# One stage for the out-projection and the FFN head of a two-layer transformer kernel, and raw weights asked for piece by piece

## The chip, the cores and the metric

The kernel runs on one core of a Trainium2 chip. The metric is device microseconds of one execution; before the change the median of three runs is 1880.46 us (1876.26 to 1881.61). One further execution was profiled: 1877.46 us, of which the span from its first to its last instruction is 1875.7 us. PE is TensorE, ACT ScalarE, DVE VectorE, POOL GpSimd; SP only issues DMAs.

## The reference, cut to what matters

Four batches of 512 tokens, width 512, fp32. Two layers, each attention and a feed-forward network (FFN). Layer 0, the projections of layer 1's attention and its softmax are not touched. What follows them is:

```
attn = attn.reshape(b, n, 512);  x = x + attn @ Wout + bout           # layer 1 attention, its end
xn = layernorm(x)
g = xn @ Wg.T;  u = xn @ Wu.T                                          # DFF = 1408 = 11 x 128
x += silu(g) * u @ Wd.T
for e in top2(softmax(xn @ Wr.T)), weight we:                          # 8 experts, rank 16
    h = silu(g + xn@Ag[e].T@Bg[e].T*2) * (u + xn@Au[e].T@Bu[e].T*2)
    x += we * (h @ Ad[e].T @ Bd[e].T * 2)
```

## The kernel before, in words

An fp32 product is made of fp32r halves: a matrix is split into HI (a rounding copy, on ACT) and LO (the rest, a subtraction on DVE or POOL), and each product takes three matmuls (HI HI, HI LO, LO HI). "A product of twelve" below is four blocks of 128 in depth times these three, 128 x 512 out. A matrix that must be turned first is turned on PE as 128 x 128 transposes, four to a PSUM bank, and ACT and DVE split it out of the bank.

The part that the change touches comes in this order.

- **Attention** (`phase_rope_attention1`, L1676). 32 groups of four heads. POOL divides each group's sums and writes them to `attn`, laid out by group (`normalise`, L1740). Wout comes in raw.
- **Out-projection** (`phase_out1`, L1968). ACT and DVE split Wout. Then, for each of 16 token tiles in a hardware loop over the batches (`pe.Fori`, L2001): ACT gathers the tile's rows out of `attn` (L2024), PE turns them, ACT and DVE split them, PE makes the product of twelve, DVE adds it to x and takes statistics.
- **FFN** (`phase_ffn1`, L2072). Small matrices (Ag, Au, Wr, Bd) are loaded, turned and split once. Then a loop over two halves of two batches each (L2244). Each half has a *head* (normalise, turn and split the eight token tiles; router; top two of the experts on DVE; masks of 128 expert-rank columns made by DVE and turned on PE by `turn_masks`, L2289; the products with Ag and Au, masked and split into `am`), 22 *steps*, and a *tail* (masks turned again, the accumulated low-rank rows masked and split, the product with Bd per tile, the output stored).
- **The steps.** A half goes through the 11 blocks f of DFF, and per block through its two batches c. A step (`tile`, L2340) on PE: product of twelve for g; transposes of one piece of block f+1's raw weights (`prep`); product of twelve for u; the previous step's down product (twelve); the low-rank additions for one expert choice (`lora`, six); another `prep`; the previous step's low-rank down product (six); `lora` of the other choice (six). ACT makes silu and HI, DVE the product with u and the sums into x, POOL LO.
- **The raw weights.** Gate, up, down and lora pieces of block f come by six DMAs on one semaphore. SP issues all six when all four pieces of the block before are turned (L2204). PE waits for all six ahead of the first of them:

```
sp.wait_ge(prep_.filled, START + (h * NF + f) * PREP)      # L2204, then six DMAs, L2205 to L2211
if part == 0:
    pe.wait_ge(raw_in, (h * NF + f + 1) * LOADS * DMA)     # L2232
```

The order on each engine is written out by hand; nothing plans it.

Of the kernel before, what the change touches and what calls it, by code (L numbers as in the profile page):

```python
# [1259 lines left out]
def phase_qkv1(nc, io, x, ident, stats, experts, early):  # L1260
# [20 lines left out]
    with ExitStack() as ctx:  # L1281
# [16 lines left out]
        wq = sb("wq", [P, 2, DK, 2, 2, P], FP32R)  # L1298
# [6 lines left out]
        sinT, cosT = sb("sinT", [P, 2, S]), sb("cosT", [P, 2, S])  # L1305
        ctxT = sb("ctxT", [P, 2, CK, S], FP32R)
        xn = sb("xn", [P, TPB, D])
        xnT = sb("xnT", [P, 2, DK, S], FP32R)
        y_in = early.y_in
        qk = sb("qk", [P, RING, 2, 2, S], FP32R)  # L1310
# [365 lines left out]
def phase_rope_attention1(nc, io, x, ident, attn, wout, early):  # L1676
# [7 lines left out]
    with ExitStack() as ctx:  # L1684
# [48 lines left out]
        @block.gpsimd  # L1733
        def _(pool):

            for s in range(early.SLOTS, RING):
                early.set_ones(nc.gpsimd, kM[s], slot_set[s], lambda done: pool.wait_ge(slot_set[s], done))
            pool.wait_ge(bout_in, DMA)

            def normalise(g):  # L1740
                pool.wait_ge(rinv_made, g + 1)
                nc.gpsimd.tensor_tensor(attn[:, g, :, :], sums[g % 2][:, :, 0:HD],  # L1742
                                        rinv[g % 2][:].unsqueeze(2).to_broadcast([P, KT * GROUP, HD]), ALU.mult).then_inc(out_done, 1)

            for g in range(GROUPS):
                if g < TILES:
                    nc.gpsimd.tensor_tensor(x[:, g, :], x[:, g, :], bout[:], ALU.add)
                normalise(g)

        @block.sync  # L1750
        def _(sp):
# [10 lines left out]
            sp.dma_start(wout.raw[:], io["L1_xattn_Wout"].rearrange("(k p) n -> p k n", p=P)).then_inc(wout.loaded, DMA)  # L1762
# [197 lines left out]
class OutWeights:  # L1960


    def __init__(self, nc, ctx):
        self.raw = ctx.enter_context(nc.sbuf_tensor("wout_raw", [P, DK, D], FP32))
        self.loaded = ctx.enter_context(nc.semaphore("wout_in"))


def phase_out1(nc, io, x, ident, stats, attn, wout):  # L1968

    from contextlib import ExitStack  # L1970
    with ExitStack() as ctx:
        def sb(name, shape, dt=FP32):
            return ctx.enter_context(nc.sbuf_tensor(f"o_{name}", shape, dt))

        def ps(name, shape):
            return ctx.enter_context(nc.psum_tensor(f"o_{name}", shape, FP32))

        def sem(name):
            return ctx.enter_context(nc.semaphore(f"o_{name}"))

        w = sb("w", [P, 2, DK, D], FP32R)
        rows = [sb(f"rows{i}", [P, D]) for i in range(2)]
        aT = [sb(f"aT{i}", [P, 2, DK, P], FP32R) for i in range(2)]
        tp = [ps(f"tp{i}", [P, D]) for i in range(2)]
        y_ps = [ps(f"y{i}", [P, D]) for i in range(2)]
        t_ = Split(nc, ctx, "ot")
        w_hi, w_split, rows_ready, y_ready, y_added = (
            sem("w_hi"), sem("w_split"), sem("rows_ready"), sem("y_ready"), sem("y_added"))
        block = ctx.enter_context(nc.Block())

        @block.tensor
        def _(pe):
            start_counts(pe, t_.filled)
            def out_product(tile, t):

                pe.wait_ge(t_.split, START + tile + 2)
                pe.wait_ge(y_added, START + tile)
                product(nc, y_ps[t % 2][:], [([aT[t % 2][:, h, k, :] for h in (HI, LO)],
                                              [w[:, h, k, :] for h in (HI, LO)]) for k in range(DK)]).then_inc(y_ready, 1)

            with pe.Fori(0, B) as b:  # L2001
                for t in range(TPB):
                    tile = b * TPB + t

                    pe.wait_ge(rows_ready, tile + 1)
                    pe.wait_ge(t_.split, START + tile)
                    transposes(nc, t_, tp[t % 2], [rows[t % 2][:, k * P:(k + 1) * P] for k in range(DK)], ident)
                    if t == 0:
                        pe.wait_ge(w_split, DK)
                    if t:  # L2010
                        out_product(tile - 1, t - 1)
                out_product(b * TPB + TPB - 1, TPB - 1)

        @block.scalar
        def _(act):
            act.wait_ge(wout.loaded, DMA)
            for k in range(DK):
                nc.scalar.activation(w[:, HI, k, :], wout.raw[:, k, :], ACT.Copy).then_inc(w_hi, 1)
            with act.Fori(0, B) as b:
                for t in range(TPB):  # L2020
                    tile = b * TPB + t

                    act.wait_ge(t_.filled, START + (tile - 1 if t else b * TPB))
                    nc.scalar.activation(rows[t % 2][:].rearrange("p (g c) -> p g c", g=HEADS // GROUP),  # L2024
                                         attn[:, ds(b * (HEADS // GROUP), HEADS // GROUP), t * GROUP:(t + 1) * GROUP, :]
                                         .rearrange("p g a c -> p g (a c)"), ACT.Copy).then_inc(rows_ready, 1)
                    split_hi(nc, act, t_, tile, aT[t % 2][:, HI], tp[t % 2][:].rearrange("p (k c) -> p k c", k=DK))

        @block.vector
        def _(dve):  # L2030
            start_counts(dve, t_.split, y_added)
            dve.sem_inc(t_.split, 1)
            dve.sem_inc(y_added, 1)
            for k in range(DK):
                dve.wait_ge(w_hi, k + 1)
                nc.vector.tensor_tensor(w[:, LO, k, :], wout.raw[:, k, :], fp32(w[:, HI, k, :]), ALU.subtract).then_inc(w_split, 1)

            def add(tile, t):
                dve.wait_ge(y_ready, tile + 1)
                nc.vector.tensor_tensor(x[:, ds(tile, 1), :], y_ps[t % 2][:].rearrange("p (a c) -> p a c", a=1),  # L2040
                                        x[:, ds(tile, 1), :], ALU.add).then_inc(y_added, 1)

            def out_stats(tile):

                dve.wait_ge(y_added, START + tile + 2)
                tile_stats(nc, stats, x, tile)

            with dve.Fori(0, B) as b:
                for t in range(TPB):
                    tile = b * TPB + t  # L2050
                    split_lo(nc, dve, t_, tile, aT[t % 2][:, LO], tp[t % 2][:].rearrange("p (k c) -> p k c", k=DK), aT[t % 2][:, HI])
                    if t >= 2:
                        out_stats(tile - 2)
                    if t:
                        add(tile - 1, t - 1)
                out_stats(b * TPB + TPB - 2)
                add(b * TPB + TPB - 1, TPB - 1)
                out_stats(b * TPB + TPB - 1)


def phase_rope1(nc, io, x, ident, stats, experts):
    from contextlib import ExitStack
    with ExitStack() as ctx:
        early = AttentionInputs(nc, ctx)
        phase_qkv1(nc, io, x, ident, stats, experts, early)
        attn = ctx.enter_context(nc.sbuf_tensor("attn", [P, GROUPS, TPB * GROUP, HD], FP32))
        wout = OutWeights(nc, ctx)
        phase_rope_attention1(nc, io, x, ident, attn, wout, early)
        phase_out1(nc, io, x, ident, stats, attn, wout)


def phase_ffn1(nc, io, x, ident, stats):  # L2072

    from contextlib import ExitStack
    ER = E1 * R1
    NF = DFF // P  # L2080
    HALVES = 2
    CH = B // HALVES
    HT, HTOK = CH * TPB, CH * S
    STEPS = NF * CH
    PREP = 4
    USES = TPB + 2
    gate_dram, up_dram, down_dram = io["L1_ffn_Wg"], io["L1_ffn_Wu"], io["L1_ffn_Wd"]
    out_dram = io["out"].rearrange("b (t p) d -> p (b t) d", p=P)
    with ExitStack() as ctx:
# [9 lines left out]
        xnT = sb("xnT", [P, 2, DK, HTOK], FP32R)  # L2099
        agT, auT = sb("agT", [P, 2, DK, ER], FP32R), sb("auT", [P, 2, DK, ER], FP32R)  # L2100
        wrT = sb("wrT", [P, 2, DK, E1], FP32R)
        bdT = sb("bdT", [ER, 2, D], FP32R)
        wr_raw = sb("wr_raw", [E1, D])
        gate_raw, up_raw, down_raw = sb("gate_raw", [P, D]), sb("up_raw", [P, D]), sb("down_raw", [P, DK, P])
        lora_raw = sb("lora_raw", [P, 3, P])
        gateT = [sb(f"gateT{s}", [P, 2, DK, P], FP32R) for s in range(2)]
        upT = [sb(f"upT{s}", [P, 2, DK, P], FP32R) for s in range(2)]
        downT = [sb(f"downT{s}", [P, 2, D], FP32R) for s in range(2)]
        loraT = [sb(f"loraT{s}", [P, 2, 3, P], FP32R) for s in range(2)]
        rl = sb("rl", [P, S])  # L2110
        logits = sb("logits", [P, HT, E1])
        shifted = sb("shifted", [P, HT, E1])
        rev = sb("rev", [P, HT, E1])
        hots = sb("hots", [P, HT, 4, E1])
# [575 lines left out]
```

## Time and profile before

| | us |
|---|---|
| median of three runs | 1880.46 |
| the profiled execution | 1877.46 |
| its span | 1875.7 |
| PE busy | 1663.6 (89%) |
| DVE busy | 1111.9 (59%) |
| ACT busy | 819.4 (44%) |
| POOL busy | 430.0 (23%) |
| mean granted TensorE clock | 0.941 of full |

The busy shares are averages over stages that differ. The table is read only to see which engine leads; what a stage is bound by stands in its own windows, in the waits ahead of PE, and in the order of PE's instructions. "PEld" is the loading of stationary operands, which overlaps the matmuls. Idle time of an engine that is not the last one in a stage costs nothing.

### The profile page before, as it was taken

The numbers are of one execution on the slowest core, as the hardware profiler recorded it, in microseconds if no ns is written. First come the engines' busy times: TensorE is split into PE (matmuls) and PEld (weight loads), VectorE is DVE, ScalarE is ACT, GpSimd is POOL, SyncE is SP. The second block draws the span as 40 slices with busy tenths as digits, with TensorE's granted clock in tenths as the row PEclk, the third lists the DMA queues.
The fourth block names the chain that finished last, engine by engine and source line by source line (L and its number), as shares of the span: only waits on it lengthen the run. The fifth ranks groups of instructions, "written<-read, shape, count | busy, mean of one in ns | idle before, by whom it ended". The sixth has DMA issues, their size and how long they took to land. (4 is left out here: it accounts for less than half of the span.)

```text
span 1875.7 us, 27784 instructions
## 1 busy us (share of the span) xinstructions
PE 1663.6 (89%) x8787; PEld 1220.7 (65%) x8787; DVE 1111.9 (59%) x1999; ACT 819.4 (44%) x1304; POOL 430.0 (23%) x394
## 2 busy tenths in 40 slices
PE   6978599999578869999999896899999888999997
PEld 5767599999456623334333374687778657778785
DVE  5876522222277668888988354554555565555555
ACT  4653223333244328777788722433333324333332
POOL 1210122222256621111000000322222203232221
PEclk8999599999788859999999897999999989999998
DMA  8995045742347542222222002011110030110101
GB/s 289 341 347 176 29 155 177 264 173 80 114 150 235 162 137 69 70 69 69 70 69 69 2 0 60 22 39 25 42 42 21 1 88 22 42 42 21 42 21 45
DMA packets 135840, 182.56 MB, mean 97 GB/s; under 512 B 62560, under 2 KB 83040, under 8 KB 130864
## 3 DMA queue, kind: packets, MB, share of 16 engines
q1 hardware_dynamic: 129488, 160.65, 27.3%
q0 software_dynamic: 6240, 20.45, 3.2%
q8 instruction: 65, 1.06, 0.2%
q14 instruction: 47, 0.39, 0.1%
HBM read 253.41 MB, written 61.21 MB: 168 GB/s over the span
## 5 line engine op out<-in xcount | busy, mean ns | idle before, releaser
L1926 DVE TENSOR_REDUCE r_top<-r_ring 128x1 f32<-128x512 f32 x512 | 324.1, 681 | 34.2 <-PE r_ring L1823 29.8
L1909 ACT ACTIVATE r_probs<-r_st 128x1024 f32<-128x1024 f32 x256 | 248.1, 1022 | 48.1 <-PE r_st L1810 45.5
L2482 POOL TENSOR_TENSOR f_hidS<-f_work,f_hidS 128x512 fp32r<-128x512 f32 x132 | 170.6, 1293 | 416.8 <-ACT f_hidS L2442 416.8
L48 PE MATMUL m_bank<-w_place,m_xT 128*128 x936 | 168.2, 329 | 3.4 <-DVE m_xT L1189 3.1
L2599 DVE TENSOR_TENSOR f_work<-f_work,f_u 128x512 f32<-128x512 f32 x132 | 90.8, 688 | 133.9 <-PE f_u L48 74.0
L2437 ACT ACTIVATE f_work<-f_g 128x512 f32<-128x512 f32 x132 | 79.0, 598 | 182.7 <-PE f_g L56 125.7
L48 PEld LDWEIGHTS m_bank<-w_place,m_xT 128*128 128x128 f32 x936 | 153.5, 191 | 7.7 <-issue 4.3
L2442 ACT ACTIVATE f_hidS<-f_work 128x512 fp32r<-128x512 f32 x132 | 83.4, 632 | 169.3 <-DVE f_work L2599 169.3
L1844 PE MATMUL r_out<-r_probs,early_v 128*17 128x512 f32 x1024 | 135.6, 601 | 0.5 <-ACT r_probs L1909 0.4
L48 PE MATMUL f_u<-f_xnT,f_upT 128*128 128x512 f32 x528 | 131.7, 398 | 0.0
L48 PE MATMUL f_g<-f_xnT,f_gateT 128*128 128x512 f32 x528 | 126.9, 389 | 0.0
L48 PE MATMUL f_y<-f_downT,f_hidS 128*128 128x512 f32 x528 | 126.8, 389 | 0.0
L1823 PE MATMUL r_ring<-early_slots 48*128 48x512 f32 x256 | 108.2, 507 | 17.3 <-PEq L1281 12.7
L2581 DVE TENSOR_TENSOR x_tokens<-f_y,x_tokens 128x512 f32 x176 | 120.2, 692 | 0.0
L48 PEld LDWEIGHTS f_g<-f_xnT,f_gateT 128*128 128x128 f32 x528 | 99.1, 188 | 20.7
L48 PEld LDWEIGHTS f_y<-f_downT,f_hidS 128*128 128x128 f32 x528 | 99.1, 188 | 20.6
L1823 PEld LDWEIGHTS r_ring<-early_slots 48*128 48x128 f32 x256 | 44.9, 196 | 99.0 <-DVE r_top L1926 81.2
L48 PEld LDWEIGHTS f_u<-f_xnT,f_upT 128*128 128x128 f32 x528 | 96.2, 188 | 19.0
L1823 PE MATMUL r_ring<-r_kM,r_qS 48*128 48x512 f32 x256 | 104.1, 476 | 3.0 <-DVE r_top L1926 0.7
L1194 DVE TENSOR_TENSOR m_hT<-m_bank,m_hT 128x384 fp32r<-128x384 f32 x39 | 21.8, 558 | 137.8 <-ACT m_hT L1027 105.7
L1823 PEld LDWEIGHTS r_ring<-r_kM,r_qS 48*128 48x128 f32 x256 | 43.0, 187 | 85.5 <-DVE r_top L1926 78.9
L1742 POOL TENSOR_TENSOR attn<-r_sums,r_rinv 128x256 f32<-128x256 f32 x32 | 19.9, 621 | 343.3 <-DVE r_rinv L1942 343.3
(345 smaller groups left out, 3024.2 us busy)
## 6 DMA issues: line engine op xcount, KB each, us to landing
w_place<-expert_split SPq DMA_DIRECT2D x72, 1408.0 KB
w_place<-expert_split SPq DMA_DIRECT2D x36, 1024.0 KB
expert_split<-w_place SPq DMA_DIRECT2D x10, 1408.0 KB, 8.9
w_place<-expert_split SPq DMA_DIRECT2D x36, 384.0 KB
early_slots<-y_rows SPq DMA_DIRECT2D x16, 512.0 KB, 6.0
k_split<-q_qk SPq DMA_DIRECT2D x32, 256.0 KB
q_split<-q_qk SPq DMA_DIRECT2D x32, 256.0 KB
w_raw<-in_L_ffn_down_proj SPq DMA_DIRECT2D x8, 704.0 KB, 7.2
```

What stands on the lines that cost most here:

```text
L48: last = nc.tensor.matmul(out, l, r, start=(i == 0), stop=(i == len(passes) - 1))
L1194: nc.vector.tensor_tensor(hT[:, i % 2, LO], bank[1][:, 0:FT * P].rearrange("p (j c) -> p j c", j=FT), fp32(hT[:, i % 2, HI]), ALU.subtract ...
L1742: nc.gpsimd.tensor_tensor(attn[:, g, :, :], sums[g % 2][:, :, 0:HD], rinv[g % 2][:].unsqueeze(2).to_broadcast([P, KT * GROUP, HD]), ALU.mu ...
L1823: nc.tensor.matmul(ring(place(q, h))[:], qS[s][rows, h // 2, q * P:(q + 1) * P], kM[s][rows, h // 2, :], start=True, stop=True).then_inc(m ...
L1844: last = nc.tensor.matmul(out_ps[h * PAD:h * PAD + VCOLS, :], v[:, k, g, h * VCOLS:(h + 1) * VCOLS], probs[k][:, h, :], start=(k == 0), st ...
L1909: nc.scalar.activation(probs[k][:, 2 * pair:2 * pair + 2, :], st_ps[pair][:], ACT.Exp, scale=SCALE).then_inc(exp_done, 1)
L1926: nc.vector.reduce_max(top[g % 2][:, q, h:h + 1], ring(place(q, h))[:], AXIS_X).then_inc(max_read, 1)
L2437: nc.scalar.activation(hid(c, var), g_ps[c][:], ACT.Silu).then_inc(silu_done, 1)
L2442: nc.scalar.activation(hidS[c][:, var, HI, :], hid(c, var), ACT.Copy).then_inc(hid_hi, 1)
L2482: nc.gpsimd.tensor_tensor(hidS[c][:, var, LO, :], hid(c, var), fp32(hidS[c][:, var, HI, :]), ALU.subtract).then_inc(hid_split, 1)
L2581: nc.vector.tensor_tensor(x[:, at, :], ring(c, i)[:].rearrange("p (a c) -> p a c", a=1), x[:, at, :], ALU.add).then_inc(y_added, 1)
L2599: nc.vector.tensor_tensor(hid(c, var), hid(c, var), u_ps[c][:], ALU.mult).then_inc(hid_done, 1)
```

## The change

Three things are rearranged; the arithmetic stays.

1. **Storage.** `attn`, raw Wout and split Wout are allocated ahead of the QKV phase, whose temporaries now lie in them. `attn` is laid out by token tile, so POOL writes each group to its final place and no gather on ACT is left. POOL also splits Wout, in groups 16 to 19 of the attention.
2. **One stage `phase_out_head`** over four batches in the order 2, 3, 0, 1, unrolled, software-pipelined by batch: iteration j has batch j's out-projection, batch j-1's normalisation, router and choice, and batch j-2's masks and Ag/Au products. POOL normalises. A mask is now a product of the chosen rows with a 32 x 128 selection matrix (six matmuls of 512 columns a batch) instead of 32 transposes a half, twice. Batches 2 and 3 have their turned xn and `am` (2 MB each) stored to DRAM, all batches the two masks of the tail. The first block's raw weights are turned at the end.
3. **One stream of 44 steps.** `phase_ffn1` starts at the first g product and goes on from half 0 to half 1 without a head; SP loads xn and `am` of batches 2 and 3 back over those of 0 and 1. The tail's masked delta (`make_delta`, `delta_rows`) of batches 0 and 1 lies inside steps 22 to 25; raw pieces have a semaphore each, and each is asked for when its own predecessor is turned.

```diff
+class FfnState:
+    ORDER = (2, 3, 0, 1)
...
-            def load(h, f):
-                sp.wait_ge(prep_.filled, START + (h * NF + f) * PREP)
...
+            for part in range(late.PARTS):
+                late.load_raw(sp, 1, part)
+            load_mask(0)
+            for w in range(1, SLOTS_W - 1):
+                for part in range(late.PARTS):
+                    sp.wait_ge(prep_turned, (w - 1) * late.PARTS + part + 1)
+                    late.load_raw(sp, w + 1, part)
+                if w == NF - 1:
+                    load_rows(0)
+                    load_rows(1)
+                if w == NF:
+                    load_mask(1)
+                if w == NF + 1:
+                    load_mask(2)
+                    store_rows(0, 0, TPB)
+                if w == NF + 2:
+                    store_rows(1, 0, TPB)
+            store_rows(2, 0, TPB)
+            load_mask(3)
...
+            def load_rows(c):
+                last = STEPS_H - CH + c
+                sp.wait_ge(up_ready, 3 * last + 1)
+                sp.dma_start(fp32(late.xnT[:, c].rearrange("p h k n -> p (h k n)")), late.x_dram[c]).then_inc(x_in[c], DMA)
+                sp.wait_ge(up_ready, 3 * last + 3)
+                sp.dma_start(fp32(late.am[:, c].rearrange("p i k h n -> p (i k h n)")), late.am_dram[c]).then_inc(am_in[c], DMA)
```

PE's order in the new stage (left out under `j == 0` are four transposes of the constants, `turn_const`, and under `j == B` the four `prep` of the first block):

```diff
+            turn_rows(0, 0)
+            turn_rows(0, 1)
+            for j in range(B + 2):
+                if j < B:
+                    out_product(j, 0)
+                    turn_rows(j, 2)
+                    out_product(j, 1)
+                    turn_rows(j, 3)
+                    out_product(j, 2)
+                    out_product(j, 3)
+                if j == 0:
...
+                if j == B:
...
+                if 1 <= j <= B:
+                    for t in range(TPB):
+                        turn_x(j - 1, t)
+                if j >= 2:
+                    turn_hots(j - 2)
+                if 1 <= j <= B:
+                    router(j - 1)
+                if j >= 2:
+                    masks(j - 2)
+                if 1 <= j <= B:
+                    turn_logits(j - 1)
+                if j + 1 < B:
+                    turn_rows(j + 1, 0)
+                    turn_rows(j + 1, 1)
+                if j >= 2:
+                    lora_rows(j - 2)
```

ACT follows the same order: `row_hi`, `normed_hi` x 4, `deviation` (Sqrt), `hot_rows_hi`, `copy_router`, `copy_masks` x 4, `gaps` (Exp), `row_hi` x 2 of the next batch, `masked_hi` x 4. DVE: `add`, `add_stats` and `row_lo` of the four tiles, `variance`, `normed_lo` x 4, `hot_rows_lo`, `reciprocals`, `route` (the top two, a chain of some twenty small operations), `row_lo` x 2, `mask_rows` x 4. PE's end of the steps:

```diff
+            down(STEPS - 1, SLOTS_W - 1, CH - 1)
+            delta_rows(CH)
+            down_lora(STEPS - 1, SLOTS_W - 1, CH - 1, TPB)
+            delta_rows(CH + 1)
```

## Rows read from the trace of the kernel before

**Rows 1.** Windows by stage: stretch, length, busy (count) per engine, clock, DMA share, GB/s.

```profile
1064.00:1129.00 65.00, 55.45 (x256) 44.40 (x256) 34.69 (x52) 20.07 (x36) 0.00 (x0) 0.92 0.00 0
1129.00:1179.40 50.40, 35.10 (x175) 25.43 (x176) 26.68 (x86) 18.18 (x35) 1.02 (x1) 0.80 0.26 56
1179.40:1484.10 304.70, 292.70 (x1339) 238.59 (x1337) 164.00 (x245) 105.27 (x177) 91.99 (x71) 0.99 0.13 29
1484.10:1505.00 20.90, 12.50 (x57) 8.74 (x56) 13.65 (x21) 5.41 (x10) 0.00 (x0) 0.84 0.08 31
1505.00:1545.00 40.00, 31.14 (x160) 22.54 (x161) 23.10 (x56) 13.40 (x28) 1.04 (x1) 0.87 0.32 88
1545.00:1849.30 304.30, 292.45 (x1339) 238.47 (x1337) 164.01 (x245) 105.26 (x177) 92.00 (x71) 0.99 0.13 29
1849.30:1875.70 26.40, 12.48 (x56) 8.74 (x56) 14.31 (x22) 4.13 (x9) 0.00 (x0) 0.81 0.21 80
```

**Rows 2.** Waits: engine, line, for what: us in all, times, longest.

```profile
PE f_prep L143 <- DMA f_lora_raw<-in_L_ffn_Ad: 13.6, 18, 1.0
```

**Rows 3.** Windows of the two steps of one block.

```profile
1575.47:1589.49 14.02, 13.43 (x64) 10.84 (x62) 7.30 (x11) 4.79 (x9) 3.88 (x3) 1.00 0.22 46
1589.49:1602.57 13.08, 13.08 (x63) 10.81 (x61) 7.16 (x11) 4.64 (x9) 3.87 (x3) 1.00 0.10 31
```

**Rows 4.** Timeline of SP: start, us, instruction; first and last DMA of a block.

```profile
1627.52 0.35 SPq L2205 DMA_DIRECT2D f_gate_raw<-in_L_ffn_Wg  x1
...
1630.70 1.32 SPq L2211 DMA_DIRECT2D f_lora_raw<-in_L_ffn_Ad  x1
```

**Rows 5.** Timeline of PE in the same block, idle time before in brackets.

```profile
1629.92 2.88 PE L48 MATMUL f_g<-f_xnT,f_gateT 128*128 128x512 f32 x12
1633.56 0.65 PE L143 MATMUL f_prep<-identity,f_gate_raw 128*128 128x128 f32 x4 [0.76 <-DMA f_lora_raw<-in_L_ffn_Ad]
```

**Rows 6.** Timeline of PE, first step of half 0.

```profile
1190.66 1.62 PE L56 MATMUL f_g<-f_am,f_loraT 128*128 128x512 f32 x3 [5.14 <-DVE f_work L2599]
...
1196.95 2.91 PE L48 MATMUL f_g<-f_xnT,f_gateT 128*128 128x512 f32 x12
```

**Rows 7.** Timeline of PE in the out-projection.

```profile
1070.06 4.76 PE L48 MATMUL o_y<-o_w,o_aT 128*128 128x512 f32 x12
1074.66 0.60 PE L143 MATMUL o_tp<-identity,o_rows 128*128 128x128 f32 x4
1075.02 3.00 PE L48 MATMUL o_y<-o_w,o_aT 128*128 128x512 f32 x12
...
1078.21 5.74 PE L48 MATMUL o_y<-o_w,o_aT 128*128 128x512 f32 x24
1083.79 0.60 PE L143 MATMUL o_tp<-identity,o_rows 128*128 128x128 f32 x4
...
1098.24 0.60 PE L143 MATMUL o_tp<-identity,o_rows 128*128 128x128 f32 x4
```

**Rows 8.** Timeline of DVE: one LO split; first and last operation of a choice.

```profile
1145.54 0.69 DVE L134 TENSOR_TENSOR f_xnT<-f_g,f_xnT 128x512 fp32r<-128x512 f32 x1 [0.47 <-ACT f_xnT L128]
...
1163.69 0.18 DVE L2509 COPY f_logits<-f_u 128x32 f32<-128x32 f32 x1
...
1169.59 0.22 DVE L2544 TENSOR_TENSOR f_hots<-ft_hot,ft_w 128x64 f32<-128x64 f32 x1
```

**Rows 9.** Groups of instructions: busy us, mean ns, idle before.

```profile
L2471 POOL TENSOR_TENSOR f_am<-f_work,f_am 128x512 fp32r<-128x512 f32 x8 | 11.9, 1511 | 181.3 <-ACT f_am L2429 181.3
L97 ACT ACT_TABLE_LOAD x1 | 1.3, 1283 | 6.9 <-PEq L1971 6.9
```

**Rows 10.** A window of layer 0 in which DMA loads run back to back.

```profile
270.00:275.00 5.00, 5.00 (x30) 4.58 (x30) 1.77 (x3) 1.67 (x4) 0.97 (x1) 1.00 0.99 377
```

**Rows 11.** Timeline of PE at the end of the kernel.

```profile
1845.06 2.88 PE L48 MATMUL f_y<-f_downT,f_hidS 128*128 128x512 f32 x12
```

**Rows 12.** The output's stores (1 MB each), from issue to landing.

```profile
DMA to landing us min/median/max: 4.3/4.4/5.4
```

More of the change, by code:

```diff
@@ L1991, in _, with turn @@
         @block.tensor
         def _(pe):
[L1993 to L2001, printed above, removed]
-                for t in range(TPB):
[L2003 to L2012, printed above, removed]
+            def turn(bank, ins, done):
+                at = 0
+                for a in ins:
+                    n_rows, n_cols = a.shape[0], a.shape[1]
+                    last = nc.tensor.transpose(bank[0:n_cols, at:at + n_rows], a, ident[0:n_rows, 0:n_rows])
+                    at += n_rows
+                last.then_inc(done, 1)
@@ L2014, in _, with row_hi @@
         @block.scalar
         def _(act):
[L2016 to L2019, printed above, removed]
-                for t in range(TPB):
[L2021 to L2027, printed above, removed]
+            def row_hi(j, t):
+                act.wait_ge(rows_turned, TPB * j + t + 1)
+                wait_count(act, y_ready, TPB * j + t - 1)
+                nc.scalar.activation(aT[:, t % 2, HI], tp[t % 2][:].rearrange("p (k c) -> p k c", k=DK), ACT.Copy).then_inc(rows_hi, 1)
@@ new lines, in gaps, with masked_hi @@
+            def gaps(j):
+                act.wait_ge(gap_ready, j + 1)
+                nc.scalar.activation(shifted[:], shifted[:], ACT.Exp).then_inc(gap_exp, 1)
+                nc.scalar.activation(top.e[:], top.gap[:], ACT.Exp).then_inc(gap_exp, 1)
+            def masked_hi(j):
+                c = j % 2
+                for q in range(4):
+                    act.wait_ge(a_masked, 4 * j + q + 1)
+                    if j >= 2:
+                        act.wait_ge(am_out[c], DMA)
+                    nc.scalar.activation(late.am[:, c, q // 2, q % 2, HI, :], work[:, q, :], ACT.Copy).then_inc(am_hi, 1)
@@ L2179, in tiles @@
[L2179 to L2189 removed]
+        mask_in, acc_clear = sem("mask_in"), sem("acc_clear")
+        z_ready, z_hi, z_split, stored = sem("z_ready"), sem("z_hi"), sem("z_split"), sem("stored")
@@ new lines, in prep, with ring_wait @@
+            def prep(f, part):
+                pe.wait_ge(late.raw_in[part], (f + 1) * late.LOADS[part] * DMA)
+                wait_count(pe, prep_split, (f - 1) * late.PARTS + part)
+                ins, _, _ = late.part(f, part)
+                for k, a in enumerate(ins):
+                    last = nc.tensor.transpose(prep_ps[:, k * P:(k + 1) * P], a, ident[:])
+                last.then_inc(prep_turned, 1)
+            def ring_wait(use):
+                wait_count(pe, y_added, use - 2)
@@ new lines, in _ @@
+            for step in range(STEPS):
+                w, c = step // CH, step % CH
+                if w == NF:
+                    pe.wait_ge(x_in[c], DMA)
+                wait_count(pe, prep_split, w * late.PARTS)
+                wait_count(pe, hid_done, 3 * (step - 1))
+                product(nc, g_ps[c][:], [([late.gate(w, h, k) for h in (HI, LO)], [late.xnT[:, c, h, k, :] for h in (HI, LO)])
+                                         for k in range(DK)]).then_inc(gate_ready, 1)
+                if w + 1 < SLOTS_W:
+                    prep(w + 1, 2 * c)
+                product(nc, u_ps[c][:], [([late.up(w, h, k) for h in (HI, LO)], [late.xnT[:, c, h, k, :] for h in (HI, LO)])
+                                         for k in range(DK)]).then_inc(up_ready, 1)
+                if step:
+                    down(step - 1, (step - 1) // CH, 1 - c)
+                lora(step, w, c, 1)
+                if w + 1 < SLOTS_W:
+                    prep(w + 1, 2 * c + 1)
+                if step:
+                    down_lora(step - 1, (step - 1) // CH, 1 - c)
+                if step > STEPS_H and z_made(step - 1) is not None:
+                    delta_rows(z_made(step - 1))
+                lora(step, w, c, 2)
```

1081 lines of the change are left out of this document (597 added, 484 removed).

## The prediction

> **What bounds the kernel now.** I read the windows by stage first [rows 1]. In the two step stretches (304.7 and 304.3 us) PE is busy 292.7 and 292.5 us at clock 0.99: PE bounds them, and only its gaps can go. In the out-projection, the two heads and the two tails PE is busy 55.5 of 65.0, 35.1 of 50.4, 31.1 of 40.0, 12.5 of 20.9 and 12.5 of 26.4 us, at clocks of 0.80 to 0.92: there chains through ACT and DVE end last. Then the waits: PE stands 18 times for the raw weights [rows 2]. Of a block's two steps the one that waits takes 14.02 us, the other 13.08 [rows 3]; they hold the same 54 matmuls and eight against seven transposes (0.12 us by the 0.36 from four transposes to the next product [rows 7]), so a wait costs 0.85 to 1.0 us with its restart. The cause is in the order of issue: the six DMAs start at 1627.52, the last is issued at 1630.70, PE needs them at 1632.8 [rows 4, 5].
>
> **The raw weights.** Each piece is now asked for when its predecessor is turned, a whole block (26 us) before it is needed. The wait goes 18 times: 18 x 0.99 = **-18**. Without the wait PE is next: its matmuls follow at once in the step that has no wait. Bounds: -13.6 (the idle time alone [rows 2]) to -19.
>
> **First step.** Before it takes from 1179.4 to 1196.95, 17.5 us [rows 1, 6], with PE waiting 5.14 us because DVE is still masking and splitting `am`. Now `am` is ready. I count g 4.7 (slow clock after the barrier, as 1070.06 to 1074.66 [rows 7]), prep 0.4, u 2.8, DVE's product 1.2, lora 1.4, prep 0.4, silu and product of the second choice 0.7, lora 1.4: 13. **-4.5** (bounds -7 to 0).
>
> **Between the halves.** Removed: the last step's down part of half 0, 4.1 us (12 + 6 matmuls), the tail 20.9, and the first step of half 1, which ends as the other did, 17.4: 42.4. The head (40.0) is counted below. Added: a full step, 13.2; eight raw pieces' work that block 10 now has, 1.8; two deltas of twelve matmuls, 5.6; 0.5 for DVE, which has four adds and a mask more in steps 22 to 25 (7.2 us busy of 13.1 now [rows 3], about 12 then). And a new wait. SP is in order: for `load_rows(1)` it waits until step 21's last up product, the very end of half 0, issues 2 MB of `am`, and only then asks for block 12's gate piece. PE wants that piece 2.8 us into step 22. Loads run at up to 377 GB/s [rows 10], so 2.1 MB take 5.6 us, plus issue and landing (PE had a block's pieces 2.1 us after the last issue [rows 4, 5]): 9 us after the step's start, a wait of 6, and 1.9 for the slow clock after it (4.6 instead of 2.8 for a product [rows 7]): 8. Sum 29, so **-13**. Bounds of the new wait: 0 (the piece overtakes) to 16 (behind x and `am` both). The xn and `am` loads themselves have 13 to 21 us each and are hidden by the steps.
> The Trainium skill, DMA: Bandwidth & Descriptors (Anatomy of one DMA), gives 2.0 us + bytes / 436 GB/s for a DMA on another issue path, as an estimate 6.8 us for 2.1 MB; by it the wait would be 5 instead of 6.
>
> **The new stage against the old out-projection and heads.** Old: 1064.0 to 1179.4 and 1505 to 1545, 155.4 us. New, by following PE's order and its waits:
> - Start: no Wout split and no gather, first product 3 us in instead of 6. Products of batch 0: four at 2.8 and two turns at 0.36, 12, and 1.9 for the slow first: 14.
> - Gap to batch 1: DVE has add, statistics, variance, the four constants' LO and the reciprocals ahead of `row_lo`: 5.8.
> - Batch 1: products 12. Then turn_x: the first two at once, the others only when DVE, held by add, statistics and variance for 2.5 us, has split two tiles (ACT, then DVE, 0.69 for DVE's half [rows 8]); router from 6.0, ending 8.8; logits copied and turned by 10.2; the choice on DVE 6.1 before ([rows 8], 64 columns; 32 now); `row_lo` 0.7, next product at 17.4. With the clock down after 6 idle us, 1.9: 31.3.
> - Batch 2: the same, with masks (2.0, as the fourth waits for a copy) and lora_rows (24 matmuls, 5.5) filling the choice's time: 12 + 18.5 = 30.5.
> - Batch 3: 12, 11.2 to the logits, 5.5 lora_rows: 28.7.
> - j = 4: ACT is busy with `masked_hi` until 4 us later, so prep stalls 5 us; prep and turn_x end at 11.8, router 4.7 at the slow clock, masks and logits 2.4, lora_rows 5.5: 24.4.
> - j = 5, nothing beside it: choice 1, hots turned, split and multiplied 5.9, lora_rows 7 at a clock partly low, masking 1.5, HI 1, POOL's two LO at 1.5 [rows 9] 3: 19.9. Barrier 0.9.
>
> Sum 158.5, **+3**. The old stage's 16 transposes of masks a half, twice, and 2.4 us a batch lost at each loop turn (14.45 from 1083.79 to 1098.24 against 12.0 [rows 7]) do go; what takes their place is a serial chain a batch (split, router, choice, split) with only two batches' work to lie beside it. PE's work here is about 98 us at full clock; it is idle for the rest. Bounds: 140 (chains shorter, gaps filled) to 183 (the 12.3 us of PE work behind each batch's chain at half clock, and 1 us more in each hand-over).
> Hidden, and what it costs without cover: POOL's Wout split (8 operations, up to 1.5 us [rows 9], POOL nearly idle in the attention); stores of 9 MB (no engine waits, except for mask buffers); four more Sqrt and four Exp loads on ACT, 1.28 us each [rows 9], which fall where ACT waits anyhow; 10 us if all were exposed. The attention itself I leave at 0, -1 to +2.
> The Trainium skill, ScalarE: Activation LUTs (What ACT_TABLE_LOAD costs), puts a switch at 2.66 us with a drain; eight exposed would be 21. By rows 9 the load takes 1.28. This is the page's rule that speaks against the change.
>
> **Tail.** Old: 30.6 from the last down product at 1845.06 to the end [rows 11]. New: down 2.7; make_delta(2) 4.4, during which PE idles; delta 4.7 at the slow clock; down_lora 1.4. Then mask 3, whose load SP issues only behind the 1 MB store of batch 2, lands about 15.5 after the down product; delta chain 3.5, product 4.7, last add, store (4.4 a MB [rows 12], less for a quarter) and end 4.5. Sum 2.7 + 28 = 30.7: **0** (-4 to +4).
>
> **Sum** against the profiled execution: -18 - 4.5 - 13 + 3 + 0 = -32.5; 1877.5 - 32.5 = 1845. That execution is 3.0 us below the median of the three runs, inside their spread; I put the median at **1846**.
>
> **Rivals.**
> - *The stage's chains overlap better* than I follow them (140 to 148 us): 1832. For it: DVE is busy 0.53 and ACT 0.31 of the old stages [rows 1]. Against: DVE's own order puts `route` ahead of `row_lo`.
> - *The reload holds longer*: xn and `am`, 8 MB through one queue while raw pieces wait behind; each block boundary at 11 and 12 loses 8 more: 1860. For it: SP is in order. Against: the loads are spread over 26 us.
> - *The change doesn't do what it says for the raw weights*: the wait was PE's own pipeline at the piece's turn, not the data. Then -18 is lost: 1864. Against: the step with two preps and no wait takes 13.08.
> - *Slower*: the new stage runs at 1.2 GHz. Its PE use after each batch's products is under half for 12 us, and the old head shows 0.80 [rows 1] with a product of twelve at 4.6 instead of 2.8 after a pause [rows 7]. If the clock stays low through whole batches, the 84 us of PE work after batch 0 take up to 84 more, of which I put 45 on the path: 1891. It decides from 35 us on. Against: the old out-projection, with 1.8 us gaps each batch, keeps the full clock.
>
> **Chances.** Forecast (1836 to 1856) 0.55, better overlap 0.16, longer reload 0.12, no gain on raw weights 0.06, slow clock 0.05, other mishaps between 1860 and 1880 0.06. The range 1829 to 1866 takes in the first three and most of the fourth. About 0.3% (5.6 us) is what a measurement here tells from no change: faster 0.92, same 0.03, slower 0.05.
>
> **What would show it.** Raw weights: no PE wait for `lora_raw`, 26.3 us a block instead of 27.1 to 27.4. Reload: one wait of 5 to 8 us of PE for a gate piece in step 22, none for xn. Stage: 150 to 165 us from the attention's last transposes to the first g, PE idle 4 to 7 us ahead of each `out_product(j, 0)` for j = 1, and at `turn_x(j, 2)`. Tail: DVE idle 4 us for mask 3. Wrong: a stage under 145 or over 170 us, or blocks that still take 27.

## The result, and the profile after

The changed kernel takes 1845.9 us (median of four runs, 1844.3 to 1850.5) beside 1881.0 for the kernel before (1876.3 to 1881.7): ratio 0.9822, 95% interval 0.9806 to 0.9838. The forecast was 1846, range 1829 to 1866. Timed again later, beside the experiments, the ratio was 0.9794 (0.9773 to 0.9815), 1847.2 against 1885.0.

The profiled execution is the slowest of the four: 1850.5 us, span 1848.7. Its windows by stage (stretch, length, busy per engine with count, clock, DMA share, GB/s) answer to [rows 1]:

```profile
1068.33:1225.84 157.51, 124.72 (x551) 90.64 (x552) 77.62 (x213) 53.63 (x99) 32.13 (x33) 0.87 0.22 79
1225.84:1239.68 13.84, 12.57 (x44) 9.62 (x45) 2.76 (x4) 5.28 (x8) 5.44 (x3) 0.78 0.50 140
1239.68:1515.76 276.08, 276.08 (x1292) 228.14 (x1291) 151.78 (x231) 97.92 (x169) 82.19 (x64) 1.00 0.21 58
1515.76:1537.22 21.46, 15.27 (x63) 12.31 (x62) 7.31 (x11) 4.78 (x9) 3.88 (x3) 0.84 0.46 144
1537.22:1569.24 32.02, 32.02 (x149) 26.11 (x147) 26.51 (x38) 10.37 (x19) 8.37 (x6) 1.00 0.39 114
1569.24:1817.17 247.93, 247.93 (x1155) 204.96 (x1153) 134.88 (x205) 86.66 (x149) 73.51 (x57) 1.00 0.15 35
1817.17:1848.70 31.53, 15.09 (x43) 10.87 (x41) 15.52 (x23) 2.01 (x4) 1.57 (x2) 0.73 0.24 83
```

They are the joined stage, the first step, steps 1 to 21, step 22 (the first of the second half), steps 23 and 24 with their deltas, the rest of the steps, the tail. In three of them (276.08, 32.02, 247.93 us) PE's busy time equals the length; in [rows 1] the two step stretches had 12 us of gaps each. The waits of PE from the attention's end on (line, for what: us in all, times, longest) have no `lora_raw` any more [rows 2]; what is left is the stage, the reload, the barrier ahead of the first g (`f_g`, 5.0) and the tail. The seven largest are:

```profile
PE f_ring L48 <- DVE wout_split L2777: 13.3, 2, 9.2
PE h_y L48 <- DVE late_weights L2405: 7.9, 3, 4.8
PE h_tp L2171 <- DVE late_xnT L2434: 7.3, 4, 2.0
PE f_prep L2632 <- DMA wout_raw<-in_L_ffn_Wg: 6.2, 1, 6.2
PE f_g L48 <- PEq L2059: 5.0, 1, 5.0
PE h_tp L2234 <- issue: 3.8, 1, 3.8
PE h_y L2171 <- DVE late_weights L2501: 3.1, 1, 3.1
```

The two steps of a block, read from where PE starts each step's g (timeline, start and length), take 13.21 and 13.08 us, 26.29 a block, against 14.02 and 13.08 [rows 3]:

```profile
1608.62 2.89 PE L48 MATMUL f_g<-late_xnT,late_weights 128*128 128x512 f32 x12
1621.83 2.88 PE L48 MATMUL f_g<-late_xnT,late_weights 128*128 128x512 f32 x12
1634.91 2.89 PE L48 MATMUL f_g<-late_xnT,late_weights 128*128 128x512 f32 x12
```

The reload at the change of half, SP's requests and then PE:

```profile
1508.80 0.32 SPq L2588 DMA_DIRECT2D late_xnT<-late_x_dram  x1
1515.96 0.32 SPq L2590 DMA_DIRECT2D late_am<-late_am_dram  x1
1516.32 0.69 SPq L2042 DMA_DIRECT2D wout_raw<-in_L_ffn_Wg  x1
```

```profile
1515.76 2.88 PE L48 MATMUL f_g<-late_xnT,late_weights 128*128 128x512 f32 x12
1524.84 1.12 PE L2632 MATMUL f_prep<-identity,wout_raw 128*128 128x128 f32 x4 [6.19 <-DMA wout_raw<-in_L_ffn_Wg]
1525.60 4.50 PE L48 MATMUL f_u<-late_xnT,late_weights 128*128 128x512 f32 x12
```

SP asks for the gate piece only after the second `am`, which waits for the last product that reads its buffer. PE wants the piece 2.7 us into step 22, gets it 6.19 us later, and runs the next product of twelve in 4.50 us instead of 3.0. From its request to PE's start the piece takes 8.5 us, with 2 MB of `am` ahead of it in the same queue; the 21 gate pieces of the kernel take 2.4 us at least, 2.6 in the median and 8.5 at most, this one (DMA issues: count, KB, median us from issue to landing):

```profile
wout_raw<-in_L_ffn_Wg SPq DMA_DIRECT2D x21, 256.0 KB, 2.6
```

The spans differ by 27.0 us. The milestones of both traces (attention's last turn, first g, end of the first step, last down product, end) divide that among the prediction's terms:

| stretch | predicted | measured |
|---|---|---|
| up to the attention's end | 0 | +4.1 |
| joined stage against out-projection and first head | +43.1 | +42.3 |
| first step | -4.5 | -3.7 |
| first step's end to last down product | -71.3 | -70.6 |
| tail | +0.1 | +0.9 |
| sum | -32.6 | -27.0 |

The second and fourth lines hold one move: the second half's head (40.0 us) was forecast inside the stage and leaves the steps, so +3 is 43.1 - 40.0, and -71.3 is -18 (waits) - 42.4 - 40.0 + 29.1.

### The profile page after: what moved, and what is told of

It reads as the page before. It is cut to its first block and busy times, and to the rows that moved or that the text cites. A ratio compares the mean times of both kernels' runs of the same rounds, so it can differ in the third digit from the quotient of the medians.

```text
span 1848.7 us, 25581 instructions
## 1 busy us (share of the span) xinstructions
PE 1657.8 (90%) x8699; PEld 1217.9 (66%) x8699; DVE 1088.1 (59%) x2001; ACT 808.5 (44%) x1283; POOL 458.6 (25%) x425
## 5 line engine op out<-in xcount | busy, mean ns | idle before, releaser
L1937 DVE TENSOR_REDUCE r_top<-r_ring 128x1 f32<-128x512 f32 x512 | 324.1, 682 | 35.8 <-PE r_ring L1834 31.5
L2719 ACT ACTIVATE attn<-f_g 128x512 f32<-128x512 f32 x132 | 79.1, 599 | 192.1 <-PE f_g L56 132.2
L2793 DVE TENSOR_TENSOR attn<-attn,f_u 128x512 f32<-128x512 f32 x132 | 90.8, 688 | 121.4 <-PE f_u L48 67.0
L2748 POOL TENSOR_TENSOR wout_split<-attn,wout_split 128x512 fp32r<-128x512 f32 x66 | 85.8, 1300 | 215.2 <-ACT wout_split L2723 215.2
L2748 POOL TENSOR_TENSOR f_hidS<-attn,f_hidS 128x512 fp32r<-128x512 f32 x66 | 85.7, 1298 | 204.2 <-ACT f_hidS L2723 204.2
L48 PE MATMUL f_g<-late_xnT,late_weights 128*128 128x512 f32 x528 | 129.6, 395 | 5.0 <-PEq L2059 5.0
L48 PE MATMUL f_u<-late_xnT,late_weights 128*128 128x512 f32 x528 | 133.6, 402 | 0.0
L2761 DVE TENSOR_TENSOR x_tokens<-f_ring,x_tokens 128x512 f32<-128x512 f32 x176 | 120.2, 692 | 0.0
L48 PEld LDWEIGHTS f_g<-late_xnT,late_weights 128*128 128x128 f32 x528 | 100.7, 191 | 26.5 <-issue 5.4
L48 PEld LDWEIGHTS f_u<-late_xnT,late_weights 128*128 128x128 f32 x528 | 97.3, 191 | 19.4
L48 PE MATMUL m_bank<-w_place,m_hT 128*128 (+1 forms) x351 | 90.8, 403 | 1.4 <-DVE m_hT L1194 1.4
```

The costliest lines, as they stand in the source:

```text
L48: last = nc.tensor.matmul(out, l, r, start=(i == 0), stop=(i == len(passes) - 1))
L1937: nc.vector.reduce_max(top[g % 2][:, q, h:h + 1], ring(place(q, h))[:], AXIS_X).then_inc(max_read, 1)
L2719: nc.scalar.activation(hid[:, c, var, :], g_ps[c][:], ACT.Silu).then_inc(silu_done, 1)
L2748: nc.gpsimd.tensor_tensor(hidS[c][:, var, LO, :], hid[:, c, var, :], fp32(hidS[c][:, var, HI, :]), ALU.subtract).then_inc(hid_split, 1)
L2761: nc.vector.tensor_tensor(x[:, at, :], ring(use)[:], x[:, at, :], ALU.add).then_inc(y_added, 1)
L2793: nc.vector.tensor_tensor(hid[:, c, var, :], hid[:, c, var, :], u_ps[c][:], ALU.mult).then_inc(hid_done, 1)
```

## The experiments

Times are medians; "before" is 1885.0 in the first group of four (17 runs), 1885.0 in the second (9) and 1885.6 in the third (9). The changed kernel was timed in the second group (1847.2); runs of the other groups are compared with it too, as "before" agrees within 0.6 us.

**e1_pieces_only.** The kernel before, with the raw weights' part of the change alone (SP's loop over the blocks is unrolled for it).

```
- sp.wait_ge(prep_.filled, START + (h * NF + f) * PREP)      # all four turned
- sp.dma_start(gate_raw ...).then_inc(raw_in, DMA); ...      # six, one semaphore
+ turned(0); sp.dma_start(gate_raw ...).then_inc(raw_in[0], DMA)
+ turned(1); sp.dma_start(up_raw ...).then_inc(raw_in[1], DMA)
+ ...
```

> The kernel before, with one part of the change alone: the six raw low-rank pieces of an FFN step are asked for one by one, each with its own semaphore, as their buffers come free. If the 13.6 us for which TensorE stood ahead of the first prep product, 18 times, was the landing of pieces asked for too late, 17 to 18 steps lose about 1 us each: 16 to 19 us faster than before, about 1863. The rival, that the 1 us was TensorE's own pipeline or the VectorE copies and not the transfer, gives 0: about 1880.

1862.8 us (1861.0 to 1867.0), ratio 0.9887 (0.9861 to 0.9912): 22 us faster. PE waits for no lora piece, and its steps start 13.21 and 13.09 us apart, as in the changed kernel:

```profile
1566.95 2.89 PE L48 MATMUL f_g<-f_xnT,f_gateT 128*128 128x512 f32 x12
1580.16 2.89 PE L48 MATMUL f_g<-f_xnT,f_gateT 128*128 128x512 f32 x12
1593.25 2.89 PE L48 MATMUL f_g<-f_xnT,f_gateT 128*128 128x512 f32 x12
```

From the first low-rank product to the last down product the profile has 1828.10 - 1192.14 = 635.96 us, against 1845.06 - 1190.66 = 654.40 before [rows 6, 11]: 18.4. So the wait was the data, and it was worth 18 in that execution; the medians gave 22, above the 16 to 19 expected.

**e2_pieces_undone, e2_second_look.** The changed kernel with that part undone.

```
- for part in range(late.PARTS):
-     sp.wait_ge(prep_turned, (w - 1) * late.PARTS + part + 1)
-     late.load_raw(sp, w + 1, part)
+ sp.wait_ge(prep_turned, w * late.PARTS)
+ for part in range(late.PARTS):
+     late.load_raw(sp, w + 1, part)
```

PE waits for all four pieces ahead of the first, at the reload too.

> The changed kernel with that one part undone: the six raw pieces are asked for together once all four pieces of the step have been turned, and TensorE waits for all of them ahead of the first prep product. Theory: 19 to 21 us slower than the changed kernel, about 1866 (one such wait per step again). Rival, that the gain of the whole change came from the joined stage and the better overlap: 0 to 5 us slower, about 1848.

1880.8 us (14 runs, 1868.6 to 1886.2): 34 us slower than the changed kernel, more than any theory had. The rival is out, but the size was open. The profile (1868.6, the fastest of the 14) loses 26.3 us in its steps: 607.80 against 581.49 from first low-rank to last down product. Of these 23.7 are waits for the pieces. The one at the reload is 8.91 us instead of 6.19, and the other 18 in that stretch sum to 20.9, 1.16 each, where the kernel before has 0.76 each [rows 2]; those of the second half are the longer ones (0.90 to 2.11 us, against 0.50 to 1.09). So undoing the part costs more here than it won there. A second profile was taken for the rest; the steps of the first, "about 604" below, are 607.80 us as measured:

> A second profile of the kernel in which the raw pieces are asked for together. Its first profile lay 12 us under the median of its times, and the steps of that profile lost 26 us against the changed kernel's, while the medians differ by 33. If the short waits also cost clock in some executions, a slower profile has blocks with a granted clock under 1.00 (or products of twelve over 2.9 us) in the steps; if the rest is of the stages before, the steps take again about 604 us and the difference lies ahead of them.

1874.8 us, steps 610.96: 3.2 more than the first. The waits are the same in sum; the first profile's, then the second's:

```profile
PE f_prep L2634 <- DMA wout_raw<-in_L_ffn_Ad: 30.7, 20, 8.9
```

```profile
PE f_prep L2634 <- DMA wout_raw<-in_L_ffn_Ad: 30.3, 20, 8.9
```

The clock is not. The same step in the two, with the wait in brackets and the product after it:

```profile
1705.53 0.63 PE L2634 MATMUL f_prep<-identity,wout_raw 128*128 128x128 f32 x4 [2.11 <-DMA wout_raw<-in_L_ffn_Ad]
1705.91 3.01 PE L48 MATMUL f_u<-late_xnT,late_weights 128*128 128x512 f32 x12
```

```profile
1707.32 0.63 PE L2634 MATMUL f_prep<-identity,wout_raw 128*128 128x128 f32 x4 [2.01 <-DMA wout_raw<-in_L_ffn_Ad]
1707.70 4.58 PE L48 MATMUL f_u<-late_xnT,late_weights 128*128 128x512 f32 x12
```

A stall of 2 us cost 1.6 us of slow product besides in one execution and nothing in the other; in the second profile it happened twice (again after a wait of 2.11 us), which is 3.1 of the 3.2. So the clock theory holds for these 3.2 us. The median is 6 us above even this profile, and that rest has not been seen in a trace. It stays open.

**before_second_look.** The kernel before, profiled again.

> A second profile of the kernel before, for the same question: taking its 18 waits away alone won 22 us by the medians, 18 by the length of its steps. If short waits cost clock in some executions, the two step stretches take more than 304.7 and 304.3 us here and show a granted clock under 0.99; if not, they take 304 to 305 again.

1885.6 us. The windows of the steps behind each half's first step have a clock of 1.00 in both profiles, so here the clock theory fails; but the steps take 1852.81 - 1192.75 = 660.06 us, 5.7 more than in the first profile, and the waits are longer than in [rows 2]:

```profile
PE f_prep L143 <- DMA f_lora_raw<-in_L_ffn_Ad: 18.7, 18, 1.3
```

Neither theory of this expectation named that: the time until the pieces are there differs between executions (0.52 to 0.94 us of wait at the first block, 0.89 to 1.31 at the fourth). Against this profile e1 wins 24.1 us in its steps, against the first 18.4; its median lies between.

**e3_reload_order.** SP's order at the reload.

```
- if w == NF - 1: load_rows(0); load_rows(1)      # x0, am0, x1, am1
- (next turn of the loop) raws(NF, (0, 1, 2, 3))
+ load_x(0); raws(NF, (0, 1)); load_am(0); raws(NF, (2,)); load_x(1); raws(NF, (3,)); load_am(1)
```

> The changed kernel with the order of SyncE's requests changed at the reload of the gate's second-half weights: each raw gate or up piece is asked for ahead of the store or accumulator load that waits for a late product, where its buffer is already free. In the changed kernel TensorE stood 6.19 us for the reloaded piece, and the step after it ran 21.46 us against 13.2. Theory, a request held up behind others in SyncE's order: 7 to 9 us faster, about 1838. Rival, that the transfer itself or the accumulators' loads are what comes last: 0 to 2 us.

1837.2 us (1836.1 to 1842.0), ratio 0.9749 (0.9727 to 0.9771), 10.0 under the changed kernel's 1847.2. The gate piece is now asked for 20 us ahead of the step and before `am` (SP, then PE), and step 22 runs through at full clock in 13.21 us (21.46 before the edit):

```profile
1491.50 0.34 SPq L2588 DMA_DIRECT2D late_xnT<-late_x_dram  x1
1491.89 0.43 SPq L2042 DMA_DIRECT2D wout_raw<-in_L_ffn_Wg  x1
1496.02 0.33 SPq L2044 DMA_DIRECT2D wout_raw<-in_L_ffn_Wu  x1
1498.78 0.33 SPq L2593 DMA_DIRECT2D late_am<-late_am_dram  x1
```

```profile
1511.68 2.89 PE L48 MATMUL f_g<-late_xnT,late_weights 128*128 128x512 f32 x12
1514.40 0.60 PE L2644 MATMUL f_prep<-identity,wout_raw 128*128 128x128 f32 x4
1514.76 3.00 PE L48 MATMUL f_u<-late_xnT,late_weights 128*128 128x512 f32 x12
...
1524.89 2.88 PE L48 MATMUL f_g<-late_xnT,late_weights 128*128 128x512 f32 x12
```

From the first step's end to the last down product: 569.2 us against 577.5. The 8.3 us came from when the piece was asked for and what lay ahead of it in the queue; the `am` load itself, which nothing sped up, stays hidden. This run doesn't tell the two apart: how much a faster `am` transfer would have won in the old order was not tested.

**e4_mask_early.** The last mask goes into an accumulator that is already free, ahead of the stores.

```
+ sp.wait_ge(z_split, 1)
+ sp.dma_start(down_acc[:, 0] ..., late.mask_dram[3]).then_inc(mask3_in, DMA)
  store_rows(2, 0, TPB)
- load_mask(3)
```

> The changed kernel with the last mask loaded early into an accumulator buffer that is already free, on a semaphore of its own, so that the tail doesn't wait for it. In the profile VectorE stood 4.95 us for that mask, and TensorE's last delta product 9.18 us behind VectorE. Theory, the mask is on the path that sets the end: 5 to 6 us faster, about 1840. Rival, that the stores of the last blocks or the split of the down delta come last at once behind it: 0 to 1 us.

1841.7 us (1836.7 to 1843.8), ratio 0.9767 (0.9746 to 0.9788). In the changed kernel's tail (VectorE, then PE):

```profile
1836.59 0.69 DVE L2772 TENSOR_TENSOR attn<-attn 128x512 f32<-128x512 f32 x1 [4.95 <-DMA attn<-late_mask_dram]
...
1840.09 5.49 PE L48 MATMUL f_ring<-late_bdT,wout_split 128*128 128x512 f32 x12 [9.18 <-DVE wout_split L2777]
```

and in this one:

```profile
1827.24 4.60 PE L48 MATMUL f_ring<-late_bdT,wout_split 128*128 128x512 f32 x12 [4.34 <-DVE wout_split L2782]
```

The tail takes 1835.0 - 1809.13 = 25.9 us against 31.5, 5.7 less, 0.9 of it the shorter delta product; the medians give 5.5. The mask was what came last.

**after_again.** The changed kernel, as the measure.

> The changed kernel itself, unaltered, as the measure for the kernels run beside it. The ratio to the kernel before should come out at 0.98 again. Its profile tells whether the 4.1 us by which the end of attention (work that the change doesn't touch) lay later in the first profile was of that one execution: then attention should end at 1062 to 1063 us here; if it is of the change, again at 1066.

1847.2 us. Attention ends at 1062.1 us here, and between 1060.5 and 1067.6 in the profiles of the other experiments, none of which touches it: the 4.1 us of the table's first line belong to the one execution. Everything behind it repeats within 0.3 us here (stage 157.26, steps 577.41). The stage doesn't do so always: in the profiles of e2 (two), e3, e4 and e7, which leave it as it is, it takes 154.64, 157.39, 156.76, 153.79 and 157.40 us. In the two short ones (154.64 and 153.79) the same products run in less time; the third of the four routers, for one, takes 2.94 and 3.38 us instead of 5.28.

**e5_rows_first.** VectorE's order in the stage's second round, and ScalarE's with it (`gaps` and `row_hi` are ScalarE's).

```
- gaps(0); row_hi(2, ...); route(0); row_lo(2, ...)
+ row_hi(2, ...); gaps(0); row_lo(2, ...); route(0)       # for j == 1 alone
```

> The changed kernel with one edit in the joined stage: in the second round of its loop VectorE makes the next batch's row halves ahead of the gaps and the routing of the batch before. In the changed kernel TensorE stood 7.9 us in 3 waits for these halves (4.80 us ahead of batch 2's product). Theory, it is VectorE's order: 3.5 to 6 us faster than the changed kernel. Rival, that routing then comes late and TensorE waits for the turned x halves instead, or the time is only the clock's: 0, or 1 to 2 us slower.

1841.0 us (1838.7 to 1844.1), 6.2 faster; the stage takes 150.53 us against 157.26. Batch 2's first product in the changed kernel (second profile), then here:

```profile
1115.29 5.49 PE L48 MATMUL h_y<-wout_split,late_weights 128*128 128x512 f32 x12 [4.79 <-DVE late_weights L2405]
```

```profile
1111.30 3.03 PE L48 MATMUL h_y<-wout_split,late_weights 128*128 128x512 f32 x12 [0.97 <-DVE late_weights L2407]
```

Of the 6.7 us, 3.8 are the wait and 2.5 this product's clock. PE waits nowhere for the routing after it. The rival's clock is thus a part of the gain, behind the wait. Which of the two engines' orders mattered more was not separated.

**e6_filled_gaps.** Extra matmuls in PE's gaps.

```
+ if j < B and t == 2: warm(j, 8)      # 8 matmuls 128x512, result not read
  turn_x(j - 1, t)
  ...
+ if j < B: warm(j, 4)
```

> The changed kernel with extra work: 12 further matmuls of 128x512 in each of three rounds of the joined stage's loop, put where TensorE otherwise waits for VectorE; nothing reads their result. The router products took 4.79, 2.94, 5.28 and 2.94 us in the four rounds, and the stage's mean granted clock was 0.87. Theory, idle TensorE costs the stage its clock: the products all take 2.9 us, 3 to 6 us faster. Rival, the clock falls for another reason, or the extra work lies on the path: 0, or up to 5 us slower.

1839.3 us (1838.0 to 1841.2), ratio 0.9755 (0.9736 to 0.9774) against 0.9794: 7.9 faster, though it does more work. The router product of the second round in the changed kernel, then here:

```profile
1103.67 4.72 PE L56 MATMUL h_r<-late_xnT,h_wrT 128*8 128x512 f32 x12 [1.50 <-DVE late_xnT L2434]
```

```profile
1103.94 2.94 PE L56 MATMUL h_r<-late_xnT,h_wrT 128*8 128x512 f32 x12 [0.58 <-DVE late_xnT L2444]
```

The stage takes 152.15 us, 5.1 less. From one batch's first product to the next's, the three rounds with extra matmuls win 2.2, 0.5 and 2.4 us. Since an unchanged stage also came out at 153.8 once, the better evidence is the times, whose ranges don't meet (1838.0 to 1841.2, and 1842.9 to 1848.5), and the router above: it takes 4.70 to 5.02 us in all nine profiles without the extra matmuls, e5 and e8 among them, and 2.94 in both with them. Idle PE did cost the stage clock; the rival is out. The expectation that all products would take 2.9 us failed: behind its 4.79 us of wait batch 2's product still takes 5.28 us, and the last `lora_rows` 7.07.

**e7_both, e8_all, e9_all_warm.** e3 and e4 together; with e5; with e6 as well.

> The changed kernel with both the changed order of requests at the reload and the early last mask. In their profiles the steps from the first one's end to the last down product took 569.2 us against 577.5, and the tail 25.9 us against 31.5. If the two don't touch each other, the sum is 13.9 us faster than the changed kernel, in time about 1833 to 1837. Rival, that the early load of the mask gets between the reordered requests: 8 to 10 us.

1831.2 us (1827.1 to 1833.6), 16.0 faster: two more than the sum of the profiles and just under the 1833 to 1837 expected, but the sum of the two medians' gains is 15.5.

> The changed kernel with the three edits that each won alone: order of requests at the reload and early last mask (together 1831.2 against 1847.2 us), and the row halves first in the second round of the stage (1841.0). They lie in three places of the kernel and share no engine's time: 1847.2 - 16.0 - 6.2 = 1825 if they add up. Rival, that the second round's edit and the rest overlap by the clock: 1828 to 1831.

1823.8 us (1821.7 to 1828.4), ratio 0.968 (0.9664 to 0.9696): the edits add up.

> The kernel with the three edits, and beside them the extra matmuls in the gaps of three rounds of the stage (their result isn't read). Alone they won 7.9 us, but part of that was the slow product of batch 2, which the edit of the second round already mends. Theory, the rest of the slow products (router of rounds 1 and 3) still goes: 3 to 5 us faster than with the three edits alone, about 1821. Rival, that the extra work now lies on the path, since the gaps are shorter: 0 to 3 us slower.

1821.9 us (1817.1 to 1824.9), ratio 0.9656 (0.964 to 0.9672). That is 1.9 us under e8 where 3 to 5 were expected, and the intervals overlap, so the times alone leave open whether the extra matmuls still help. The stage in the two profiles, e8 then e9, says that they do in the stage (mean granted clock 0.89 and 0.93, 5.2 us):

```profile
1062.30:1212.07 149.77, 120.52 (x551) 86.75 (x552) 77.07 (x213) 53.45 (x99) 32.10 (x33) 0.89 0.23 83
```

```profile
1069.36:1213.95 144.59, 124.12 (x587) 92.00 (x588) 77.36 (x213) 53.61 (x99) 32.13 (x33) 0.93 0.25 86
```

The whole span of that e9 profile is 3.2 us longer than e8's all the same, since its attention ends 7.1 us later. e9 has the lowest median, 25 us under the changed kernel and 64 under the one before; e8 reaches nearly the same without useless work, and the two aren't separated.

## Why the prediction was right, and where it was lucky

- **The raw weights (-18).** Right in mechanism and size: 18.4 by e1 against the same profile. What it lacked: one trace shows one draw of a transfer's time. The waits summed to 13.6 and 18.7 us in two executions of the same kernel, so the -18 is 18 to 24. The idle time alone would have been too little: 18.4 us went where the waits sum to 13.6.
- **First step (-4.5).** 13.84 us where I counted 13: the first product after the barrier took 5.46, not 4.7.
- **Between the halves (-13).** Right, in the parts that the trace shows: the deltas cost 2.63 and 2.97 us (32.02 for two steps of 13.2), forecast 5.6 together. The wait for the reloaded piece was forecast at 6 and measured at 6.19, with 1.5 us of slow clock behind it (forecast 1.9). One reading under it was wrong: PE had the block's pieces 2.9 us after the last issue (1630.70 to 1633.56 [rows 4, 5]), where I wrote 2.1, which is when it wanted them; the 9 us that it helped to make came out at 9.1. The 0.5 for VectorE did not appear: PE is busy for all of 32.02 us. The Trainium skill, DMA: Bandwidth & Descriptors (Anatomy of one DMA), made the wait 5 as an estimate; the measurement lies nearer to the sum from rows. What neither shows is how to remove the wait: e3 does it by the order of requests, with the transfers themselves untouched. The transfer is in the wait all the same: a gate piece asked for as late, but landing in the 2.6 us of the others, would be there at about 1518.9 (an estimate from its request at 1516.32), and PE wants it at 1518.65.
- **The stage (+3).** 157.5 us against 158.5, and part of this nearness is luck: the parts deviate more than the sum. From the start of one batch's first product to the next's I had 19.8, 31.3 and 30.5 for batches 0, 1 and 2; they took 19.3, 29.9 and 34.1, then 30.6 for batch 3 (28.7), 20.6 for the round after (24.4) and 20.6 for the last with its barrier (20.8). The errors of batches 2 and 3 are the clock. The sum has one slow product of 1.9 us, in batch 1's line; the trace has the router slow there (4.79 us), then batch 2's product (5.49) and the lora_rows behind it (7.01 instead of 5.7), and in batch 3's line the router again (5.28), which I had at full clock. These errors were cancelled by the prep stall (3.1 instead of 5) and the router (2.9 instead of 4.7) of the round after, which I had slow. The idle times named as a sign were also off: PE idles 2.54 us ahead of batch 1's product and 2.02 at `turn_x(j, 2)`, not 4 to 7; only ahead of batch 2's it is 4.80.
- **Activation tables at 0.** Right. The groups of ACT in the stage's window show six loads of 1283 ns at these two lines, where I had counted eight. PE's waits on ACT there sum to 1.2 us, and behind each of the three Exp loads (L2334) ACT waits another 1.8 to 2.7 us for VectorE, so that they lie in idle time:

```profile
L2303 ACT ACT_TABLE_LOAD x3 | 3.8, 1283 | 0.1
L2334 ACT ACT_TABLE_LOAD x3 | 3.8, 1283 | 0.1
```

  The Trainium skill, ScalarE: Activation LUTs (What ACT_TABLE_LOAD costs), puts a switch at about 1283 ns of load and 1380 ns of drain, 2.66 us; six of them exposed would be 16 us more. The trace agrees with the load's 1283 ns and shows no drain on ACT's timeline: the load at 1139.70 us starts 0.01 us after the operation before it ends, and the next operation 0.02 us after the load.
- **Tail (0).** +0.9, with mask 3 last, as forecast. The two delta products took 5.33 and 5.49 us where I had 4.7 each.
- **Attention (0).** +4.1 in one execution, 0 in the next: chance.

The median came out at the forecast to 0.1 us, and that is luck. Profile against profile the sum was 5.5 us too favourable (4.1 of it the attention). Against that the first profile of the kernel before was a quick one (1877.5 beside its median of 1881.0), and the profiled execution after the slowest of four (1850.5 beside 1845.9). The terms came out within 1 us each apart from the attention. But the attention's end (1060.5 to 1067.6 us) and the unchanged stage (153.8 to 157.5) vary by more than that between executions, so the total could be known to some 5.

Of the rivals, "longer reload" had the right place and its price stayed at the forecast's 8. "The stage runs at 1.2 GHz" was right that the clock falls there and wrong in size, since it never stays low through a whole batch: the slow instructions of the stage take about 16 us more than the same ones do at the full level (an estimate, from 3.02, 2.94 and 5.75 us for a product, a router and a lora_rows), not 84 or the 45 put on the path. The extra matmuls of e6 won back about 5 of them.

## What to carry to other kernels

Where SP issues in order, look at what each request waits for, not only at what it moves: one load that waits for a late buffer holds every request behind it, and then lies ahead of them in the queue; moving the free ones ahead won 8 us. Ask for each piece as its own buffer comes free; a wait of 0.8 to 1.0 us, 18 times, was worth 18 to 24. When both sums and medians are used, take two profiles of the kernel before: what differs between them is the precision of the sum.

## What the hardware showed unexpectedly

- The granted clock does not follow from one idle gap alone. In the changed kernel the routers of its four rounds took 4.79, 2.94, 5.28 and 2.94 us, a product of twelve being at the 2.4 GHz level in 2.9 and near the 1.2 GHz level in 5.3. The second and the third came behind the same waits of PE (2.02 us, then about 1.0). All four repeated in the second profile (4.72, 2.95, 5.28, 2.94), but in the first profile of e2, whose stage is the same, the third ran at the high level behind the same waits (2.02 and 1.02 us). The third router in the changed kernel, then in e2:

```profile
1171.66 5.28 PE L56 MATMUL h_r<-late_xnT,h_wrT 128*8 128x512 f32 x12 [0.96 <-issue]
```

```profile
1167.03 2.94 PE L56 MATMUL h_r<-late_xnT,h_wrT 128*8 128x512 f32 x12 [1.02 <-issue]
```

- 36 extra matmuls that nobody reads made the stage 5 us shorter in two pairs of profiles (157.26 to 152.15, 149.77 to 144.59), with PE's busy time in it going from 124.5 to 128.6 us only in the first pair.
- The same six DMAs let PE wait 0.5 to 2.1 us in different blocks of one execution of e2, and in the kernel before 13.6 us in sum in one execution and 18.7 in another.
